# A seeded score bank: ScalarE copies the row of maxima into PSUM ahead of the score products of the first attention

## The reference

```python
xn = _layernorm(x, gamma_media, beta_media)         # the context, 1601 rows
ln = _layernorm(latents, gamma_lat, beta_lat)       # 512 rows
q = ln @ Wq + bq
kv = jnp.concatenate([xn, ln], axis=1) @ Wkv + bkv  # 2113 rows
k, v = jnp.split(kv, 2, axis=-1)
q, k, v = (to_heads(q), to_heads(k), to_heads(v))   # 8 heads of 128, 4 batches
sim = jnp.einsum('bhid,bhjd->bhij', q * DH ** (-0.5), k)
attn = jax.nn.softmax(sim, axis=-1)
out = jnp.einsum('bhij,bhjd->bhid', attn, v)
return out.transpose(0, 2, 1, 3).reshape(b, -1, INNER) @ Wo + bo
```

## Time and profile before

| what | value |
| --- | --- |
| median of three runs | 2589.64 us (2588.78 to 2592.06) |
| the profiled execution, its own time | 2591.05 us |
| span of its profile | 2589.5 us |
| PE busy over the span | 2407.9 us, 93% |
| DVE, POOL, ACT busy over the span | 73%, 70%, 65% |
| granted PE clock, mean | 0.972 |

### The profile page before, as it was taken

How to read it: one execution, slowest core, us unless ns; L and a number is a source line. 1 busy time by engine, 2 the same in 40 slices (tenths; PEclk the granted TensorE clock), 3 DMA queues, 4 the chain that set the end, 5 groups by cost and what they waited for, 6 DMA issues and landing times. The chain is left out here.

```text
span 2589.5 us, 43858 instructions
## 1 busy us (share of the span) xinstructions
PE 2407.9 (93%) x14931; PEld 1421.3 (55%) x15058; DVE 1893.8 (73%) x3499; ACT 1673.1 (65%) x2692; POOL 1815.2 (70%) x1580
## 2 busy tenths in 40 slices
PE   5999999999999999999999579979999999869997
PEld 3455555555555555555554368844444444448886
DVE  7878777787777787777777556658888889777443
ACT  4556665556655566656566546638888888768664
POOL 2687877787777778786768656617777779737664
PEclk9999999999999999999999789989999999969998
DMA  4000000000000000000000365531211010176333
GB/s 149 1 1 1 26 1 1 1 1 1 26 1 1 1 1 1 1 1 1 1 1 1 106 145 146 116 101 43 51 27 46 23 36 16 48 216 167 51 47 68
DMA packets 90955, 108.38 MB, mean 42 GB/s; under 512 B 18866, under 2 KB 80259, under 8 KB 90707
## 3 DMA queue, kind: packets, MB, share of 16 engines
q1 hardware_dynamic: 68500, 80.57, 10.3%
q0 software_dynamic: 21696, 24.98, 6.1%
q10 hardware_dynamic: 544, 0.00, 0.0%
HBM read 68.75 MB, written 25.88 MB: 37 GB/s over the span
## 5 line engine op out<-in xcount | busy, mean ns | idle before, releaser
L417 POOL TENSOR_TENSOR a_acc<-a_acc,a_pf 128x512 f32<-128x512 f32 (+1 forms) x480 | 657.1, 1369 | 309.1 <-ACT a_pf L574 287.4
L574 ACT ACTIVATE a_pf<-a_psS 128x1024 f32<-128x1024 f32 (+1 forms) x288 | 281.2, 976 | 308.3 <-PE a_psS L717 302.4
L2176 POOL TENSOR_TENSOR c_pl<-c_pf,c_ph 128x512 f16<-128x512 f32 x320 | 375.2, 1201 | 116.6 <-ACT c_ph L2275 116.2
L869 DVE TENSOR_TENSOR a_pl<-a_pf,a_ph 128x512 f16<-128x512 f32 x448 | 430.8, 971 | 24.8 <-ACT a_ph L580 24.7
L845 DVE TENSOR_REDUCE a_mx<-a_psA 128x1 f32<-128x512 f32 x504 | 337.2, 684 | 45.8 <-PE a_psA L652 40.8
L580 ACT ACTIVATE a_ph<-a_psS 128x1024 f16<-128x1024 f32 (+1 forms) x288 | 281.0, 976 | 0.0
L2508 DVE TENSOR_REDUCE c_wf<-c_psA 128x1 f32<-128x512 f32 x384 | 246.8, 683 | 18.8 <-PE c_psA L2347 18.7
L2268 ACT ACTIVATE c_pf<-c_psS 128x1024 f32<-128x1024 f32 x192 | 197.5, 1029 | 66.3 <-PE c_psS L2381 65.1
L1431 POOL DMA_INDIRECT f_sums<-f_xn,f_sidx x78 | 144.3, 1850 | 119.4 <-DVE f_xn L1830 91.2
L840 DVE TENSOR_TENSOR a_vl<-a_psA,a_vh 128x256 f16<-128x256 f32 (+1 forms) x266 | 112.5, 423 | 142.1 <-ACT a_vh L503 139.1
L739 PE MATMUL a_psO<-a_pl,a_vh 128*128 128x512 f16 (+1 forms) x544 | 206.5, 380 | 5.1 <-POOL a_pl L435 5.1
(11 more groups left out here) (363 smaller groups left out, 6373.2 us busy)
## 6 DMA issues: line engine op xcount, KB each, us to landing
f_stage<-in_L_ffn_w SPq DMA_DIRECT2D x16, 1024.0 KB, 5.5
f_stage<-in_L_ffn_W SPq DMA_DIRECT2D x16, 1024.0 KB, 5.7
c_kst<-c_khs SPq DMA_DIRECT2D x64, 100.1 KB, 2.2
a_cx<-in_ctx SPq DMA_DIRECT2D x4, 1536.0 KB
c_cx<-in_ctx SPq DMA_DIRECT2D x12, 512.0 KB, 3.8
f_sums<-X SPq DMA_DIRECT2D x2, 2048.0 KB, 13.0
f_xrow<-f_xn SPq DMA_DIRECT2D x8, 512.0 KB, 4.4
c_kst<-c_kls SPq DMA_DIRECT2D x32, 100.1 KB, 2.2
```

Of the source, the lines that this page charges most:

```text
L417: g.tensor_tensor(acc[0:k, p, :], acc[0:k, p, :], pf[0:k, q % RF, i, :], ALU.add).then_inc(s_acc, 1)
L574: act.activation(pf[0:r, q % RF, 0:k, :], psS[q % 2][0:r, 0:k, :], ACT.Exp, scale=SCALE).then_inc(s_pF, 1)
L869: v.tensor_tensor(pl[0:r, q % RP, i, :], pf[0:r, q % RF, i, :], ph[0:r, q % RP, i, :], ALU.subtract).then_inc(s_pL, 1)
L2176: g.tensor_tensor(pl[0:r, q % RP, i, :], pf[0:r, q % RF, i, :], ph[0:r, q % RP, i, :], ALU.subtract).then_inc(s_pG, 1)
```

## The change

The fourth product leaves most score tiles. For every unit but unit 0 of each head and unit 1 of the first head (`seeded`), ACT writes the row of maxima into the two banks of `psS` before PE starts on them (`fill`), and PE's three products accumulate onto it: none of them opens the accumulation (`first` is false). To have the maxima in a form that ACT can copy, a new item R is made once a head: PE multiplies ones by `mrow` once into a bank of the ring (in place 3 of unit 8 of the head before; for the first head in place 2 of unit 0), and ACT copies the result to `mb`, 128 x 512 in 32 bits. `fill(q + 2)` stands on ACT right behind the exponential to `ph` of unit q, ahead of the items of places 2 and 3, except in unit 0 of the first head and in unit 8 of each, where it stands behind them. PE waits with the first product of a seeded unit for `s_fill` in place of `s_pH`.

```diff
-                               (6, 3, ("L", m))):
+                               (6, 3, ("L", m)), (U - 1, 3, ("R", m))):
                 at[u][p].append(what)
+        if n == 0:
+            at[0][2].append(("R", 0))
...
+    def seeded(q):
+
+        return q >= 2 and q % U > 0
+
+    def filled(q):
+        return sum(seeded(w) for w in range(q + 1))
...
+        mb = sb("mb", [P, S], F32)
...
+                elif what[0] == "R":
+                    act.wait_ge(s_it, i + 1)
+                    act.activation(mb[:, :], ps[:, :], ACT.Copy).then_inc(s_ah, 1)
+
+            def fill(q):
+
+                n, u = divmod(q, U)
+                k, r = len(UNITS[u]), rows0(UNITS[u][-1])
+                act.wait_ge(s_ah, after_act(("R", n)))
+                act.wait_ge(s_pH, q - 1)
+                act.activation(psS[q % 2][0:r, 0:k, :], mb[0:r, :].unsqueeze(1).broadcast_to([r, k, S]),
+                               ACT.Copy).then_inc(s_fill, 1)
...
                     act.activation(ph[0:r, q % RP, 0:k, :], psS[q % 2][0:r, 0:k, :], ACT.Exp,
                                    scale=SCALE).then_inc(s_pH, 1)
+                    early = 0 < q and u < U - 1
+                    if early and seeded(q + 2):
+                        fill(q + 2)
                     for what in places[2] + places[3]:
                         item(what)
+                    if not early and q + 2 < NH * U and seeded(q + 2):
+                        fill(q + 2)
...
+                elif what[0] == "R":
+                    n = what[1]
+                    pe.wait_ge(s_mrow, n + 1)
+                    ins = pe.matmul(ps[:, :], oneb[:, :], mrow[:, n % 2, :], start=True, stop=True)
...
-                triple(ps, kh[:, p, js], kl[:, p, js], qh[:, p, :], ql[:, p, :], True, False)
-                if u == 0 and i == 0:
-                    pe.wait_ge(s_mrow, n + 1)
-                ins = pe.matmul(ps, oneb[:, 0:r], mrow[:, p, :], start=False, stop=True)
+                if seeded(q):
+                    ins = triple(ps, kh[:, p, js], kl[:, p, js], qh[:, p, :], ql[:, p, :], False, True, True)
+                else:
+                    triple(ps, kh[:, p, js], kl[:, p, js], qh[:, p, :], ql[:, p, :], True, False)
+                    if i == 0:
+                        pe.wait_ge(s_mrow, n + 1)
+                    ins = pe.matmul(ps, oneb[:, 0:r], mrow[:, p, :], start=False, stop=True)
```

More of the change, by code:

```diff
@@ L165, in attention0 @@
     LAST = [max((j for j in range(max(0, i - 2 * NOPEN), i) if BANK[j] == BANK[i]), default=None) for i in range(len(ALL))]
-    N_ACT = {"Q": 1, "K": 1, "V": 1, "T": 2, "O": 2, "M": 0, "L": 0, "S": 0, "B": 0}
-    N_DVE = {"Q": 1, "K": 1, "V": 1, "T": 0, "O": 0, "M": 1, "L": 1, "S": 1, "B": 1}
+    N_ACT = {"Q": 1, "K": 1, "V": 1, "T": 2, "O": 2, "M": 0, "L": 0, "S": 0, "B": 0, "R": 1}
+    N_DVE = {"Q": 1, "K": 1, "V": 1, "T": 0, "O": 0, "M": 1, "L": 1, "S": 1, "B": 1, "R": 0}
     AH = list(itertools.accumulate(N_ACT[w[0]] for w in ALL))
@@ L178, in after_dve, with opened @@
         return FR[IDX[what]]
+    def opened(slot):
+        return max(k for k in range(len(OPEN)) if (BANK[k] - NB) // 2 == slot)
     def turned(b, group):
@@ L316, in attention0 @@
         s_mrow = sem("mrow")
+        s_fill = sem("fill")
         s_sP = sem("sP")
@@ L590, in _, with triple @@
         def _(pe):
[L591 to L595, removed]
+            def triple(out, hi, lo, xh_, xl_, first=True, last=True, onto=False):
+                pe.matmul(out, hi, xh_, start=first, stop=False, skip_group_check=onto)
+                pe.matmul(out, hi, xl_, start=False, stop=False, skip_group_check=onto)
+                return pe.matmul(out, lo, xh_, start=False, stop=last, skip_group_check=onto)
             def free(i):
@@ L601, in free @@
                     return
-                if ALL[last][0] in "TO":
+                if ALL[last][0] in "TOR":
                     pe.wait_ge(s_ah, AH[last])
@@ L702, in score @@
                 js = slice(j * P, j * P + r)
-                if i == 0:
+                if i == 0 and not seeded(q):
                     if q >= 2:
                         pe.wait_ge(s_pH, q - 1)
[L706 to L710, removed]
+                    else:
+                        last = opened(q)
                         pe.wait_ge(s_fr, FR[last])
                         pe.wait_ge(s_ah, AH[last])
+                    pe.wait_ge(s_fr, max(after_dve(("Q", n)), after_dve(("K", n, NK - 1))))
+                elif i == 0:
+                    pe.wait_ge(s_fill, filled(q))
                 ps = psS[q % 2][0:r, i, :]
-                triple(ps, kh[:, p, js], kl[:, p, js], qh[:, p, :], ql[:, p, :], True, False)
-                if u == 0 and i == 0:
-                    pe.wait_ge(s_mrow, n + 1)
-                ins = pe.matmul(ps, oneb[:, 0:r], mrow[:, p, :], start=False, stop=True)
+                if seeded(q):
+                    ins = triple(ps, kh[:, p, js], kl[:, p, js], qh[:, p, :], ql[:, p, :], False, True, True)
+                else:
+                    triple(ps, kh[:, p, js], kl[:, p, js], qh[:, p, :], ql[:, p, :], True, False)
+                    if i == 0:
+                        pe.wait_ge(s_mrow, n + 1)
+                    ins = pe.matmul(ps, oneb[:, 0:r], mrow[:, p, :], start=False, stop=True)
                 if i == len(UNITS[u]) - 1:
```

## The result

The changed kernel takes 2577.69 us (median of five runs, 2574.35 to 2580.14) against 2589.64 us before: a ratio of 0.995, interval 0.9936 to 0.9963. It is faster, by 12 us. The forecast was 2525 us, with a range from 2498 to 2557, so the kernel came out 53 us slower than forecast and 21 us outside the range.

A forecast was written before the change was run, and what follows sets the result against it. PE was taken to bound the layer: 96.3 us of products, less 7 (V), 10 (R), 8 (filled heads) and 6 (T heads), gave 65 us off 2591.05; with the median 1.4 lower, 2525 us, range 2498 to 2557.

The forecast's parts named there:

- the signs named: Listed in advance: plain heads at 39.8 to 41 us, head 3 about 1.5 us shorter, `mrow` waits in about half the heads.
- R's wait: At a head's end PE asks for `mrow` earlier: 0.86 us short in one head, 10 us over 18 heads.
- wait one: V's eviction behind unit 5's fill delays the bank for unit 6's V product: 0.35 us in 20 plain heads, 7 us.
- Heads that DVE or ACT fill: Three heads lose 1.5 us each, three 1.2, together 8 us; six heads with T items lose 1 each, 6 us.
- Rival (b): Dense end of a head: POOL operations meeting a `low` make `mrow` 0.9 us later in 31 heads; 2553 us, chance 0.20.

## Why the prediction was wrong

The forecast had the direction, and its sum missed by far: 65 us against 12. The removal was right: 478 products go, 32 come, at 0.216 us each. So were the fill's own duration (1028 ns), its being in time (no matmul waits for one between 200 and 1200 us), and POOL's additions (mean 1400 ns for those of 128 rows in that window, below the 1450 named). Three of the signs named failed: plain heads measure 41.8 to 42.5 us and not 39.8 to 41, head 3 is shortened by 0.6 us and not 1.5, and PE waits for `mrow` at R in 3 of 23 heads and not in half of them. R's wait was sized for a plain head at up to 0.86 us, and without fills it is 0.58; in the changed kernel nearly all of it is gone, because PE is already late when it comes there: 1.3 us in 1000.

**The step that failed is the sum of DVE's share**, in wait one and in "Heads that DVE or ACT fill". I worked out a single place, V of unit 6, at 0.35 us (0.47 in the head shown), and took the rest of a plain head as having margin. Three others came. In head 24 of the changed kernel PE waits 0.47 us at a rough score in unit 3, for the bank of V of unit 2; 0.83 at the V product of unit 3, for K's bank; 0.24 at an output product in unit 5, for the bank of V of unit 4; and 0.48 at the V product of unit 6. Together they are 2.0 of the 3.0 us. The largest needs no fill; it is the one that stays in the run without them. I took DVE's idle time ahead of K in unit 3, 0.89 us, as given, though it was only there because PE came later: two products less in each unit bring K forward step by step, while DVE's own work from K to K did not shrink but grew: 6.7 us without a pause in the trace without fills, against 6.5 us before (1133.71 to 1140.20) with the 0.89 of idle time in them.

**The rival was put on the wrong engine.** Rival (b) had the slowing of DVE and POOL by each other, but as POOL's lateness at `mrow`, 0.9 us a head. It acts on DVE first: `low` takes 1.56 and 1.61 us in place of 1.27 and 0.68 where PE needs K's bank. The chance of 0.20 was on a rival whose time, 2553, was also 25 us too low. The Trainium skill, "SBUF — State Buffer", section "Who interferes with whom", says that a VectorE instruction with two SBUF inputs contends with GpSimd's reads; the run with short additions agrees, with `low` at 0.68 us in both rows shown.

**The fill was priced too low.** I had 0.93 us of ACT; it is 1.15, and with its place ahead of V it costs 26 to 29 us in all where I had about 7 in the plain heads and 6 in those with T items. The T heads alone have 12 us of it. There two evictions of 0.78 us stand behind the fill and V as well, and these heads became 1.3 us slower than before, where I had them 2 us faster.

**The last two heads were counted like the others.** Their 29 products are 6.3 us of the 96.3. POOL's additions set the pace there, so they bring nothing, and with the fills the two heads took 3 us more than before. The sum had no term for this.

By the runs the 84 us between the products removed and the gain are some 29 for the fills and 55 for DVE and POOL, of which 50 lie in heads 0 to 29. Open stays how these 50 divide between the slowing and the plain amount of work. The shorter addition brings 48 of them back and the shorter reduction 29, so DVE's own amount of work is not the whole of it; but the shorter addition also takes away POOL's own lateness, and no run takes away the slowing alone.

## What to carry to other kernels

When the busiest engine gets less work, look at the engines whose waits are for it: their idle time is not spare, it is the time by which they would be late next. In a ring of three buffers work out each release of a whole period with the new spacing, and not the one that looks tightest. Copies that must only be done "some time before" belong behind the work that others wait for, and after a gain of this kind the cheap moves of order are worth trying again, since one that brings 2 us at most before brought 30 after. And read an experiment by stretch, for an edit that also reaches another stage, or a stage where another engine sets the pace, makes a cause look larger than it is.

## What was not expected of the hardware

An ACT copy of 128 x 1024 in 32 bits into PSUM, from 128 x 512 in SBUF read twice, takes 1028 ns, the same as an exponential of that size from PSUM to SBUF (1025). A DVE subtraction of 128 x 512 with both inputs in SBUF takes 0.68 us in the places shown without a POOL addition beside it, and up to 1.61 us in those beside one. A fill that waits for the semaphore of the exponential right ahead on ACT starts 0.09 us behind its end, and one that waits for the copy to `mb` right ahead starts 0.03 us behind that (453.97 to 454.00 at the end of head 8), where instructions that are ready start about 0.1 us before the end.
